# One element cleared by GpSimd between any two gathers of a graph layer

## The chip, the cores and the metric

The kernel runs on one core of a Trainium2 chip. The metric is the device time of one execution in microseconds, as the median of several runs.

## The reference

A graph of 12,500 nodes with 32 features each, and 400,000 edges, sorted by their target `dst`. Two layers, each followed by a layer norm over the 32 features with a residual:

```python
m = relu(x[src] + edge_attr)                         # layer 0: one message per edge
neigh = segment_sum(m, dst)
x = layernorm(x + (1 + eps) * x + neigh)

out_deg, in_deg = clip(count(src), 1), clip(count(dst), 1)   # layer 1
y = x * rsqrt(out_deg)
x = layernorm(x + segment_sum(y[src], dst) * rsqrt(in_deg))
```

## The kernel before

**Layer 0** (`layer_0`) takes the edges in 125 groups of 3200, as 128 partitions by J = 25 edges. Per group the feature rows of the source nodes must come from `x` in HBM. GpSimd fetches them with 25 indirect DMAs (`gathers`, L152): each takes one column of `src_t` (128 row numbers) and fetches 128 rows of 128 bytes into `rows[:, slot, j, :]`. `rows`, `src_t`, `dst_t` and `edge_t` have four slots, so a group uses slot g % 4.

Every engine runs its own program, in steps (`turns`): steps 0 to 3 are written out, then a loop of four steps a turn, then the rest. In step g VectorE and ScalarE work on the gathered rows of group g - 1:

- ScalarE copies the edge features into PSUM (L565), VectorE adds the gathered rows (L412; the first half of the group waits until all 25 gathers of it have landed, `z_rows`), ScalarE applies the relu and splits the sum into bf16 parts with VectorE (L572, L417, L576, L421).
- VectorE makes one-hot matrices from node numbers (`one_hot`, L132): `b_hot` and `key_hot` for the counts that layer 1 needs, `hi_hot` and `lo_hot` for the degree of the sources, `dst_hot` for the targets.
- TensorE multiplies, in this order: 24 products into `built` (L636), each pair of which ScalarE takes away (L587) into `stage` (a part of `big`), 25 for the histogram of sources (L641), and 25 that sum the messages by target into `agg` (L648). The last of these raises `z_agg`.
- SyncE stores `stage` to HBM (`stash`, L514), and every second step loads the indices and edge features of two groups (L489, L491).

GpSimd's own step g waits for the indices of group g, for `z_sum` (the slot of `rows` must have been read), and for `z_agg` to be at least g - 1, which is the end of TensorE's last `agg` product of step g - 1. Then it issues its 25 gathers. So the gathers of group g run beside step g of the other engines, and are used in step g + 1.

**Layer 1** (`layer_1`) has no gather in the usual case: it applies the stored counts with matmuls. GpSimd rests there. `general_sums` is a fall-back for other inputs and is skipped with these.

Of the kernel before, what the change touches and what calls it, by code (L numbers as in the profile page):

```python
# [4 lines left out]
F32, BF16, F16, I32, U32 = mybir.dt.float32, mybir.dt.bfloat16, mybir.dt.float16, mybir.dt.int32, mybir.dt.uint32  # L5
# [4 lines left out]
P = 128  # L10
# [6 lines left out]
def build(nc, x, src, dst, edge, eps, out, table, x1):  # L17
    N, D = x.shape
    E = src.shape[0]
    J = 25  # L20
# [34 lines left out]
    with ExitStack() as ctx:  # L55
        def allocators(stack):
            return (lambda name, shape, dt=F32: stack.enter_context(nc.sbuf_tensor(name, shape, dt)),
                    lambda name: stack.enter_context(nc.psum_tensor(name, [P, 512], F32)))

        sb, pb = allocators(ctx)  # L60

        def sem(name):
            return ctx.enter_context(nc.semaphore(name))
# [36 lines left out]
        s_mark = sem("s_mark")  # L100
# [48 lines left out]
        def gathers(gp, j0, j1, nodes, rows_d, src_d, s):  # L149

            for j in range(j0, j1):
                gp.indirect_dma_start(  # L152
                    rows_d[:, j, :], None, nodes,
                    bass.IndirectOffsetOnAxis(ap=src_d[:, j:j + 1].bitcast(U32), axis=0),
                ).then_inc(s, 16)
# [56 lines left out]
        def layer_0():  # L212
# [5 lines left out]
            def turns(engine, step):  # L218
                for g in range(4):
                    step(g, g, 0)  # L220
                with engine.Fori(0, fours) as i:
                    for slot in range(4):
                        step(i * 4 + (4 + slot), slot, i + 1)
                for g in range(4 + 4 * fours, G + 2):
                    step(g, g % 4, g // 4)

            def builds(g):

                return not isinstance(g, int) or g < G
# [13 lines left out]
            def loaded(engine, s, s_first, slot, use, n):  # L243

                if isinstance(use, int) and use == 1 and slot == 0:
                    engine.wait_ge(s_first, n)
                else:
                    engine.wait_ge(s[slot // 2], use * n)

            with ExitStack() as own:  # L250
                sb, pb = allocators(own)
                src_t = sb("src_t", [P, 4, J], I32)
                dst_t = sb("dst_t", [P, 4, J], I32)
                edge_t = sb("edge_t", [P, 4, J, D])
                rows = sb("rows", [P, 4, J, D])
# [33 lines left out]
                agg_bank = pb("agg")  # L289
                agg, folded = agg_bank[0:R, 0:W], agg_bank[0:DE, W:2 * W]  # L290
                taken = sb("taken", [R, W])
                sum_ps = pb("sum_ps")[:, 0:JA * D].rearrange("p (j d) -> p j d", d=D)
                built = [own.enter_context(nc.psum_tensor(f"built{k}", [P, 2, 512], F32)) for k in range(2)]
                turn = [built[0][:, k, :] for k in range(2)]
# [6 lines left out]
                z_rows = [sem(f"z_rows{k}") for k in range(4)]  # L301
# [81 lines left out]
                with nc.Block() as block:  # L383
# [143 lines left out]
                    @block.gpsimd  # L527
                    def _(gp):

                        for h in range(2):  # L530
                            gp.iota(pick_i[:, h, :], [[1, max(HT)], [0, SPAN]], base=h * HT[0], channel_multiplier=0).then_inc(s_const, 1)

                        def step(g, slot, u):
                            if builds(g):
                                loaded(gp, z_in, z_in0, slot, u + 1, IN)
                                gp.sem_inc(s_mark, 1)
                                if not isinstance(g, int) or g >= 4:

                                    gp.wait_ge(z_sum, g * 2 - 6)
                                    gp.sem_inc(s_mark, 1)  # L540
                                if not isinstance(g, int) or g >= 2:

                                    gp.wait_ge(z_agg, g - 1)
                                    gp.sem_inc(s_mark, 1)
                                gathers(gp, 0, J, x[:, :], rows[:, slot, :, :], src_t[:, slot, :], z_rows[slot])
                        turns(gp, step)

                    @block.scalar
# [677 lines left out]
        with ExitStack() as later:  # L1226
            with nc.psum_tensor("hist", [P, 512], F32) as hist_bank:
                hist = hist_bank[:, 0:C]
                layer_0()
                counts = later.enter_context(nc.sbuf_tensor("counts", [P, 2, HB + 1, C, CS], BF16))  # L1230
                finish_0()
            layer_1()
# [29 lines left out]
```

## Time and profile before

| | |
|---|---|
| median of 3 runs | 6035.83 us (6033.46 to 6036.26) |
| the profiled execution's own time | 6052.44 us |
| its span, from the first to the last instruction | 6050.5 us |
| VectorE, ScalarE, GpSimd busy in the span | 2859.8, 2724.8, 2963.9 us |
| TensorE busy in the span | 3462.7 us |
| share of the span before layer 1's matmuls begin | 4835.94 us of 6050.5 us |

Layer 0 fills about four fifths of the span. There no engine is near full: the time goes in the order in which the engines wait for each other. A row of the profile names the engine, the line of the kernel, the operation with what it writes and reads, how often, the busy time and the time that the engine stood idle before it, with what ended that idle time. "issue" means that nothing that the profile shows held the instruction. PE is TensorE, PEld its weight loads, DVE VectorE, ACT ScalarE, POOL GpSimd, SP SyncE.

### The profile page before, as it was taken

Reading aid. Unit: us, or ns where it says so; the run is one execution under the profiler, and the core shown is the slowest. Engines: PE = TensorE matmul, PEld = TensorE weight load, DVE = VectorE, ACT = ScalarE, POOL = GpSimd, SP = SyncE. Lnnn points to the kernel's source line nnn. Section 1 sums busy time; section 2 is a strip of 40 time slices with the busy share of each in tenths; the row PEclk is TensorE's granted clock in tenths of the full one; section 3 lists DMA queues with packets and bytes.
Section 4 is the critical chain, followed back from the end, with each engine's and each line's share of the span. In section 5 each row is a group of like instructions: output and inputs, shape, how many; then the busy total and the mean of one; then the engine's idle time right before and its main releaser. Section 6 shows DMA issues by size and latency. Waiting matters only on the chain. (4 is left out here: it accounts for less than half of the span.)

```text
span 6050.5 us, 72100 instructions
## 1 busy us (share of the span) xinstructions
PE 3462.7 (57%) x24270; PEld 1940.1 (32%) x24270; DVE 2859.8 (47%) x4229; ACT 2724.8 (45%) x2908; POOL 2963.9 (49%) x3134
## 2 busy tenths in 40 slices
PE   3444444444444444444444444444444499999998
PEld 1111111111111111111111111111111288888887
DVE  5444444444444444444444444444444544444444
ACT  3444444444444444444444444444444355555553
POOL 5666666666666666666666666666666300000000
PEclk7555555555555555555555555555555599999998
DMA  3232333333323333333232333333333389999996
GB/s 106 85 104 100 100 102 102 102 102 102 102 99 105 101 102 101 101 102 103 98 105 100 101 102 102 102 102 102 102 102 112 126 287 325 323 326 324 326 326 223
DMA packets 272749, 867.67 MB, mean 143 GB/s; under 512 B 93830, under 2 KB 143830, under 8 KB 256214
## 3 DMA queue, kind: packets, MB, share of 16 engines
q1 hardware_dynamic: 172718, 815.90, 36.3%
q0 software_dynamic: 100000, 51.40, 5.8%
q8 instruction: 16, 0.26, 0.0%
q14 instruction: 15, 0.11, 0.0%
HBM read 486.74 MB, written 380.33 MB: 143 GB/s over the span
## 5 line engine op out<-in xcount | busy, mean ns | idle before, releaser
L152 POOL DMA_INDIRECT rows<-in_x,src_t x3125 | 2962.2, 948 | 1806.7 <-issue 914.1
L587 ACT ACTIVATE big<-built 128x980 bf16<-128x980 f32 x1500 | 1790.6, 1230 | 2445.6 <-PE built L636 2298.7
L636 PE MATMUL built<-key_hot,b_hot 100*128 100x490 bf16 x3000 | 1475.6, 603 | 603.1 <-ACT big L587 308.2
L648 PE MATMUL agg<-dst_hot,msg 128*97 128x128 bf16 x3125 | 510.2, 289 | 1842.4 <-issue 1841.1
L412 DVE TENSOR_TENSOR sum_ps<-sum_ps,rows 128x416 f32<-128x416 f32 x250 | 144.2, 577 | 1999.4 <-DMA rows<-in_x,src_t 1994.1
L648 PEld LDWEIGHTS agg<-dst_hot,msg 128*97 128x97 bf16 x3125 | 379.7, 181 | 1955.8 <-issue 1953.6
L828 PE MATMUL applied<-counts,x_parts 128*96 128x160 bf16 x12250 | 916.8, 233 | 1.4 <-ACT counts L786 1.4
L828 PEld LDWEIGHTS applied<-counts,x_parts 128*96 128x96 bf16 x12250 | 880.8, 123 | 65.0 <-ACT counts L786 2.3
L132 DVE TENSOR_TENSOR key_hot<-iota_ps,hk_g 100x3920 bf16<-100x3920 f16 x375 | 820.8, 2189 | 0.0
L636 PEld LDWEIGHTS built<-key_hot,b_hot 100*128 100x128 bf16 x3000 | 232.8, 116 | 1699.3 <-issue 896.8
L786 ACT ACTIVATE counts<-built 128x980 bf16<-128x980 f32 x500 | 598.5, 1238 | 391.8 <-PE built L814 391.6
L417 DVE SCALAR_TENSOR_TENSOR sum_ps<-sum_ps,msg 128x416 f32<-128x416 f32 x250 | 144.2, 577 | 378.4 <-ACT msg L572 378.4
L132 DVE TENSOR_TENSOR b_hot<-iota_ps,hk_g 100x1024 bf16<-100x1024 f16 x375 | 257.9, 688 | 99.6 <-issue 76.1
L814 PE MATMUL built<-big,hi_hot 100*128 100x490 bf16 x1000 | 272.9, 374 | 32.7 <-DVE big L132 26.4
L641 PEld LDWEIGHTS hist<-lo_hot,hi_hot 128*128 128x128 bf16 x3125 | 268.5, 144 | 67.8 <-issue 64.0
L641 PE MATMUL hist<-lo_hot,hi_hot 128*128 128x98 bf16 x3125 | 275.8, 281 | 3.4 <-DVE lo_hot L132 3.4
L132 DVE TENSOR_TENSOR big<-iota_ps,hk_g 100x3920 bf16<-100x3920 f16 x125 | 273.6, 2189 | 0.0
L132 DVE TENSOR_TENSOR dst_hot<-iota_ps,rel 128x3200 bf16<-128x3200 f16 x125 | 226.7, 1814 | 0.1
L132 DVE TENSOR_TENSOR hi_hot<-iota_ps,s_hi 128x3200 bf16<-128x3200 f16 x125 | 226.7, 1814 | 0.0
L752 DVE CAST slots<-small 80x64 bf16<-80x64 f32 x125 | 27.6, 220 | 369.0 <-PE small L839 369.0
L132 DVE TENSOR_TENSOR lo_hot<-iota_ps,s_lo 128x2450 bf16<-128x2450 f16 x125 | 178.0, 1424 | 0.0
L572 ACT ACTIVATE msg<-sum_ps 128x416 bf16<-128x416 f32 x250 | 124.9, 500 | 93.7 <-DVE sum_ps L412 74.8
(130 smaller groups left out, 1543.4 us busy)
## 6 DMA issues: line engine op xcount, KB each, us to landing
stash<-big SPq DMA_DIRECT2D x125, 2940.0 KB
counts<-stash SPq DMA_DIRECT2D x250, 1470.0 KB, 8.7
rows<-in_x,src_t POOLq DMA_INDIRECT x3125
edge_t<-in_edge_attr SPq DMA_DIRECT2D x61, 800.0 KB
big<-in_dst SPq DMA_DIRECT2D x1, 1562.5 KB
big<-in_src SPq DMA_DIRECT2D x1, 1562.5 KB
src_t<-in_src SPq DMA_DIRECT2D x61, 24.8 KB
dst_t<-in_dst SPq DMA_DIRECT2D x61, 24.8 KB
```

The lines of the kernel that those rows point to most:

```text
L132: return ve.tensor_tensor(out.rearrange("p n (w t) -> p n w t", t=2), row[0:p, 0:w].rearrange("p (w t) -> p w t", t=2).unsqueeze(1).to_bro ...
L152: gp.indirect_dma_start(rows_d[:, j, :], None, nodes, bass.IndirectOffsetOnAxis(ap=src_d[:, j:j + 1].bitcast(U32), axis=0),).then_inc(s, 16)
L412: ve.tensor_tensor(half(h), half(h), rows[:, prev, j0:j1, :], ALU.add).then_inc(z_sum, 1)
L417: ve.scalar_tensor_tensor(half(h), half(h), 0.0, part(0, h), ALU.max, ALU.subtract).then_inc(z_left, 1)
L572: sc.activation(part(0, h), half(h), ACT.Relu).then_inc(z_part0, 1)
L587: sc.activation(stage[:, slot % 2, q, :, d0:d0 + 2 * SPAN].rearrange("p c (b d) -> p b c d", b=2), built[n % 2][:, :, 0:KEYS].rearrange("p ...
L636: last = te.matmul(built[n % 2][:, b, 0:KEYS], b_hot[:, r, t, :], key_hot[:, r, t, :], start=True, stop=True)
L641: last = te.matmul(hist[:, :], hi_hot[:, j, :], lo_hot[:, j, :], start=False, stop=False)
L648: last = te.matmul(agg, msg[:, j, 0:R], dst_hot[:, j, :], start=(j == 0), stop=(j == J - 1))
L786: sc.activation(counts[:, slot, HB, :, d0:d0 + 2 * SPAN].rearrange("p c (b d) -> p b c d", b=2), built[n % 2][:, :, 0:KEYS].rearrange("p b ...
L814: last = te.matmul(built[n % 2][:, b, 0:KEYS], hi_hot[:, slot, t, :], key_hot[:, slot, t, :], start=True, stop=True)
L828: last = te.matmul(applied[slot].rearrange("m (q d) -> m q d", d=CS), x_parts[:, c, :], counts[:, other, :, c, :], start=(c == 0), stop=(c ...
```

## The change

Layer 0's step on GpSimd issues its 25 gathers one by one, and after each a `memset` of one bf16 element in each of the 128 partitions of a new buffer `rest`, at column j. Each `memset` raises a new semaphore `z_rest`. Before its gathers, a group from the second on waits until all `memset`s of the groups before it are done. What is gathered, and when a group may begin, is otherwise as before.

```diff
@@ layer_0, buffers
                 taken = sb("taken", [R, W])
+                rest = sb("rest", [P, J], BF16)
+                z_rest = sem("z_rest")
@@ layer_0, GpSimd's step
                                     gp.wait_ge(z_agg, g - 1)
                                     gp.sem_inc(s_mark, 1)
-                                gathers(gp, 0, J, x[:, :], rows[:, slot, :, :], src_t[:, slot, :], z_rows[slot])
+                                if not isinstance(g, int) or g >= 1:
+
+                                    gp.wait_ge(z_rest, g * J)
+                                    gp.sem_inc(s_mark, 1)
+                                for j in range(J):
+
+                                    gathers(gp, j, j + 1, x[:, :], rows[:, slot, :, :], src_t[:, slot, :], z_rows[slot])
+                                    gp.memset(rest[:, j:j + 1], 0.0).then_inc(z_rest, 1)
```

## Rows read from the trace of the kernel before

**Rows 1.** The page: busy us of each engine, share of the span, instructions.
```profile
PE 3462.7 (57%) x24270; PEld 1940.1 (32%) x24270; DVE 2859.8 (47%) x4229; ACT 2724.8 (45%) x2908; POOL 2963.9 (49%) x3134
```

**Rows 2.** The waits, whole span: engine, line, waited for: us in total, times, longest.
```profile
DVE sum_ps L412 <- DMA rows<-in_x,src_t: 1994.1, 123, 18.4
PE agg L648 <- issue: 1841.1, 1041, 3.2
POOL rows L152 <- PE agg L648: 887.8, 123, 44.8
```

**Rows 3.** Groups of instructions on POOL from 164 to 4744 us.
```profile
L152 POOL DMA_INDIRECT rows<-in_x,src_t x3026 | 2858.8, 945 | 1727.9 <-issue 884.9 <-PE agg L648 843.1
```

**Rows 4.** Timeline of POOL: start us, us, instruction, idle before and releaser.
```profile
126.24 0.95 POOL L152 DMA_INDIRECT rows<-in_x,src_t  x1 [44.76 <-PE agg L648]
...
2019.67 0.94 POOL L152 DMA_INDIRECT rows<-in_x,src_t  x1 [6.68 <-PE agg L648]
2020.92 0.95 POOL L152 DMA_INDIRECT rows<-in_x,src_t  x1 [0.30 <-issue]
...
2049.66 0.95 POOL L152 DMA_INDIRECT rows<-in_x,src_t  x1 [0.30 <-issue]
2057.68 0.94 POOL L152 DMA_INDIRECT rows<-in_x,src_t  x1 [7.07 <-PE agg L648]
...
4742.97 0.94 POOL L152 DMA_INDIRECT rows<-in_x,src_t  x1 [6.41 <-PE agg L648]
```

**Rows 5.** Timeline of PE, the end of one step.
```profile
2035.60 2.25 PE L641 MATMUL hist<-lo_hot,hi_hot 128*128 128x98 bf16 x25
2037.65 0.84 PE L648 MATMUL agg<-dst_hot,msg 128*97 128x128 bf16 x6
2039.83 0.27 PE L648 MATMUL agg<-dst_hot,msg 128*97 128x128 bf16 x1 [1.34 <-issue]
...
2053.33 0.27 PE L648 MATMUL agg<-dst_hot,msg 128*97 128x128 bf16 x1 [1.83 <-issue]
2055.43 1.44 PE L648 MATMUL agg<-dst_hot,msg 128*97 128x128 bf16 x12 [1.83 <-issue]
```

**Rows 6.** Timeline of PE, the first such products, and some of the preparation.
```profile
77.00 1.07 PE L367 MATMUL built<-ident,big 125*100 125x125 f32 x4 [2.46 <-issue]
...
123.31 2.12 PE L648 MATMUL agg<-dst_hot,msg 128*97 128x128 bf16 x25
```

**Rows 7.** Timeline of DVE about the same step.
```profile
2036.11 0.55 DVE L421 TENSOR_TENSOR msg<-sum_ps,msg 128x384 bf16<-128x384 f32 x1
2053.55 0.60 DVE L412 TENSOR_TENSOR sum_ps<-sum_ps,rows 128x416 f32<-128x416 f32 x1 [16.89 <-DMA rows<-in_x,src_t]
```

**Rows 8.** Stretches: us, busy by engine, granted clock, DMA share, GB/s.
```profile
2044.00:2048.00 4.00, 0.53 (x2) 0.32 (x2) 0.00 (x0) 0.00 (x0) 3.08 (x4) 0.50 0.93 382
2084.00:2088.00 4.00, 0.27 (x1) 0.32 (x2) 0.00 (x0) 0.00 (x0) 3.09 (x4) 0.50 0.10 16
4820.00:6050.00 1230.00, 1177.70 (x14598) 1033.01 (x14598) 593.32 (x1281) 656.32 (x636) 0.00 (x0) 0.97 0.86 304
```

**Rows 9.** DMA queues from 400 to 4600 us: packets, MB, share.
```profile
q0 software_dynamic: 88736, 45.61, 7.3%
q14 instruction: 1, 0.01, 0.0%
```

**Rows 10.** Timeline of POOL before the first gather.
```profile
0.31 0.12 POOL L1246 MEMSET const-bfloat16-1.0<- 128x1 bf16 x1
0.34 0.12 POOL L1246 MEMSET const-uint8-127<- 128x1 uint8 x1
0.85 0.23 POOL L172 IOTA x_parts<- 128x128 int32 x1 [0.40 <-PEq L169]
1.05 0.12 POOL L173 IOTA col_i<- 128x1 int32 x1
```

**Rows 11.** Timeline of all engines in the preparation, beside early gathers.
```profile
44.03 3.49 DVE L334 TENSOR_TENSOR big<-big,c_first 125x3200 f32<-125x3200 int32 x1
44.60 4.78 POOL L152 DMA_INDIRECT rows<-in_x,src_t  x1 [0.30 <-issue]
```

**Rows 12.** Groups on DVE from 164 to 4744 us, the copies.
```profile
L391 DVE COPY hk_g<-hk_all 100x96 f16 x116 | 24.4, 210 | 3.7
```

## The prediction

> **What bounds the kernel now.** I read the page's busy times first. No engine is busy for more than 57% of the span [rows 1], so it is an order of waits that sets the time, and the waits say which. VectorE stands idle for 1994.1 us until the gathered rows are there, in 123 pieces; GpSimd, which gathers them, stands idle for 887.8 us until TensorE's last `agg` product, in 123 pieces too; and TensorE has 1841.1 us of idle time ahead of its `agg` products that nothing in the profile explains [rows 2]. These three make a ring. The timelines show one turn of it. Gathers start 1.25 us apart (2019.67, 2020.92: 0.95 of work, 0.30 of pause) and 25 of them take from 2019.67 to 2050.61, 30.94 us. GpSimd then rests 7.07 us until 2057.68 [rows 4]. In the meantime TensorE does its histogram at full pace (25 products in 2.25 us), then six `agg` products, and then goes over to one product in about 2.1 us, from 2039.83 to 2053.33 (seven of them); at 2055.43 the last twelve come in 1.44 us, to 2056.87 [rows 5]. GpSimd goes on 0.81 us later.
>
> A turn is thus 30.94 us of gathers, 4.82 us until TensorE runs free again, 1.44 us of products, 0.81 us of hand-over: 38.01 us, which is 2057.68 - 2019.67. Over the layer the first gathers of a group stand at 126.24 us (group 2) and 4742.97 us (group 124) [rows 4], 122 turns of 37.84 us on average; 30.93 of that is gathering, for GpSimd's wait is 843.1 us in 122 turns, 6.91 us each [rows 3].
>
> What slows the `agg` products is the open point. With no gather running, the same 25 products took 2.12 us at 123.31 us [rows 6]. Slow stretches are equally slow with the DMA engines at 0.93 and at 0.10 of their time, and in layer 1, without a gather, TensorE stays busy (1177.70 of 1230 us) with the DMA engines at 0.86 [rows 8]. So DMA load does not do it; GpSimd's gathering goes with it, in the preparation too (2.46 us ahead of four transposes while early gathers run [rows 6]). The granted clock is 0.50 of full speed (1.2 GHz) in both slow stretches [rows 8], but a half clock doesn't make gaps of two microseconds.
>
> A rule bears on this. The Trainium skill, Runtime: NRT & Kernel Launch, section "Instruction fetch mechanics", says that an engine's instructions are fetched by DMA in 16 KiB blocks, and that a taken branch whose target is not at hand waits for one. By it the slow products would be waiting for blocks, GpSimd's pace would have no part in it, and the time would go by the full chain alone. The trace disagrees: from 400 to 4600 us one instruction packet was moved [rows 9]. I give it no part in the sum.
>
> **The change, part by part.**
>
> *3125 memsets.* Each stands between two gathers in GpSimd's own order, and no other engine waits for it. Its cost on the path is what it adds to the 1.25 us from gather to gather; call it d. The trace has no memset behind a gather. Below: four memsets at the program's start lie 0.03 us apart (0.31, 0.34), each 0.12 us long [rows 10], and if the memset ran wholly inside the 0.30 us pause that stands before each gather [rows 4], d would be 0. It can hardly be under that, since the number of gathers and the 0.95 us of each stay. Above: the memset in full and a second pause, 0.12 + 0.30 = 0.42 us. I take 0.12 us, the memset's own row [rows 10] set end to end with the gather: a one-element iota after another instruction also shows 0.12 and no pause (1.05 [rows 10]). A group's gathers then take 25 x 0.12 = 3.0 us more, 33.9 us.
>
> *What happens with these 3.0 us.* I read the release of TensorE as tied to the end of gathering: in the turn above it comes 4.82 us after the last gather and 1.88 us after VectorE starts again at 2053.55 [rows 5, 7], and VectorE itself waits for the last gather to land. If this tie holds, the turn is the gathers plus the same 7.07 us, and all of the 3.0 us shows: 122 x 3.0 = 366 us. Group 124 is the last; its rows come 3.0 us later, and VectorE waits for them: 3 us. Groups 0 and 1 are gathered ahead of the ring, while VectorE still prepares, and GpSimd then waits 44.76 us [rows 4]; their 6 us are hidden by that.
>
> *The new wait on `z_rest`.* The last memset of a group is over about 7 us before the next group begins (the wait for `agg` covers it). Behind the wait only the gathers are queued. If the cover went, it would cost one memset, 0.12 us a group, 15 us. I take 0, with the semaphore increment beside it.
>
> *VectorE and the memset.* When VectorE worked on large buffers in the preparation, one gather took 4.78 us instead of 0.95, beside an instruction of 3.49 us [rows 11]; in the loop the mean is 945 ns [rows 3], so its VectorE work doesn't hold gathers up. The Trainium skill, SBUF — State Buffer, section "Who interferes with whom", says that copies in a two-port mode and GpSimd take a shared port in turn, whole instructions at a time. By it a memset that meets the copy of `hk_g` (210 ns [rows 12]) would wait for its end, at most once a group: 122 x 0.21 = 26 us on top. No row of the loop shows a gather so held.
>
> *Sum.* 366 + 3 = 369 us. Against the profiled execution's 6052.44 us that is 6421 us. That execution is 16.6 us above the median of the runs, so I put the median at 6405 us.
>
> **Rivals.**
>
> *The rest frees TensorE (faster).* The place is the slow stretch of the `agg` products. Suppose that gathers at 1.25 us overload something by a little: it would fill up for some time, slow TensorE, and need a while to drain after the last gather. For it: the six or seven fast products ahead of the slow ones, and the 4.82 us of drain after 30.94 us of gathers [rows 4, 5], which would be an excess of 15%, so that a pace slower by 0.19 us a gather would do away with it, and one slower by 0.12 us might put off its start past the last product, which needs only two more microseconds. Then `agg` is over long before the gathers, GpSimd is bound by itself, and the turn is 25 x (1.25 + 0.12) + 0.2 = 34.4 us: (37.84 - 34.4) x 122 = 420 us less, 5616 us. The point from which it decides: the slow stretch must be gone, and d below 6.6 / 25 = 0.26 us; beyond that the gathers alone take longer than the turn of now. Against it: TensorE stays slow for 4.8 us after GpSimd has stopped altogether [rows 4, 5], so that a pause of a tenth of a microsecond should free nothing. 0.29.
>
> *Only half shows.* The ring goes over two groups: from a step's first addition (2053.55 [rows 7]) to its `agg` end is some 42 us, and the gathers and the hand-over stand for the rest of two turns. If TensorE's release hangs on that chain rather than on the gathers' end, two turns grow by 3.0 us: 183 us more, 6219 us. Against it speaks the sudden release at 2055.43, for which I see nothing but the end of the gathers. 0.13.
>
> *A second pause.* The memset brings a pause of its own, d = 0.42: 10.5 us a group, 123 x 10.5 = 1292 us, 7328 us. Or d lies between, at 0.3: 6958 us. A slow dispatch would work like it: in the slow stretch TensorE's instructions come in steps of about 0.7 us (weight load and product, 2.1 us a pair at most [rows 5]), and were GpSimd's two instructions held to such a step, a pair would take 1.4 us, d = 0.15, close to what I took. 0.12.
>
> *Nothing on the path.* The memset lies in the 0.30 us pause: 6036 us. It would need d under 0.004 us to be within the bound below. 0.07.
>
> **How the numbers follow.** The forecast has 0.39. With its own spread of d (0.05 to 0.2 us: 154 to 615 us more) it reaches from 6190 to 6650 us. The case of a freed TensorE ends at 5616 us, or 5590 with a d of nearly 0.1; I take it in. Above, d = 0.28 gives 6897 us; beyond lies under a tenth. Range 5590 to 6900 us. What a measurement of this kernel can tell from no change is 0.2%, 12 us. Faster by more: 0.29. Within: 0.07. Slower by more: 0.39 + 0.13 + 0.12, 0.64.
>
> **What would show it.** In the timeline of GpSimd the distance from gather to gather: 1.37 us by the forecast, 1.25 if nothing shows, 1.67 with a second pause. GpSimd's wait for `agg` a group: still 6.9 us by the forecast, 5.4 if half shows, 0 if TensorE is freed. In TensorE's timeline the single `agg` products 2.1 us apart: one or two more of them by the forecast, and fewer in the burst at the end; all 25 in one row of some 2 us if it is freed. The distance of that burst from the last gather: 4.8 us if the tie holds. VectorE's wait for rows a group: 16 us now, 19 by the forecast. I am wrong if the distance from gather to gather grows and the wait for `agg` goes down by more than it grows.

## The result

The changed kernel takes 6076.46 us (median of 3 runs, 6076.15 to 6076.52) against 6035.83 us: 40.6 us more, ratio 1.0068 with a 95% interval of 1.0048 to 1.0088. The direction is the one forecast, the size is a ninth of it (369 us).

The page of the changed kernel, busy us of each engine and the costliest groups on GpSimd (in the groups: busy us, mean ns | idle before):

```profile
PE 3449.3 (57%) x24270; PEld 1937.3 (32%) x24270; DVE 2866.8 (47%) x4229; ACT 2723.6 (45%) x2908; POOL 3321.5 (55%) x6259
...
L152 POOL DMA_INDIRECT rows<-in_x,src_t x3125 | 2957.5, 946 | 1458.9 <-PE agg L657 826.4
...
L554 POOL MEMSET rest<- 128x1 bf16 x3125 | 374.9, 120 | 14.1 <-issue 12.8
```

The 3125 memsets are there, 120 ns each as taken, and GpSimd is 358 us busier [rows 1]. But the idle time ahead of the gathers fell by about as much (1458.9 us, 1806.7 before on the page's row for L152): the memsets lie in it. The timeline shows how:

```profile
1994.42 0.95 POOL L152 DMA_INDIRECT rows<-in_x,src_t  x1 [0.19 <-issue]
1995.37 0.12 POOL L554 MEMSET rest<- 128x1 bf16 x1
1995.67 0.94 POOL L152 DMA_INDIRECT rows<-in_x,src_t  x1 [0.19 <-issue]
```

From gather to gather it is 1.25 us, as before [rows 4]: the 0.12 us of memset came out of the 0.30 us pause. So the cost that I put on the path isn't there, and something else takes the 40 us. Two places stand out. One gather in some groups is late, always near the end of a group, and the profile shows no wait that held it:

```profile
1983.63 0.94 POOL L152 DMA_INDIRECT rows<-in_x,src_t  x1 [0.19 <-issue]
1984.56 0.13 POOL L554 MEMSET rest<- 128x1 bf16 x1
1986.00 0.94 POOL L152 DMA_INDIRECT rows<-in_x,src_t  x1 [1.32 <-issue]
1986.95 0.12 POOL L554 MEMSET rest<- 128x1 bf16 x1
1993.17 0.94 POOL L152 DMA_INDIRECT rows<-in_x,src_t  x1 [6.11 <-PE agg L657]
```

That was so for the last gather in 56 groups (1.21 us of idle time ahead of it on average, 0.19 otherwise) and for the one before it in 12, and in no group before the change. The other place is the preparation: TensorE's transposes and ScalarE's copies, which hand over to each other while the first 50 gathers run, got slower (2.46 us ahead of four transposes in [rows 6]). TensorE after the change:

```profile
77.71 1.07 PE L369 MATMUL built<-ident,big 125*100 125x125 f32 x4 [4.60 <-issue]
84.02 1.07 PE L369 MATMUL built<-ident,big 125*100 125x125 f32 x4 [5.24 <-ACT hk_all L561]
```

The ring then begins at 129.97 us, 3.7 us later than in [rows 4]. A turn is 38.006 us on average (122 turns), 0.164 more than 37.842, 20 us in all; gathers take 31.44 us of it (30.93 before), GpSimd's rest 6.56 (6.91). These two profiled executions differ by 24.1 us only (6076.52 against 6052.44); the one of before was 16.6 us above its median.

One memset was itself held up, in the preparation and not in the ring. It took 1.78 us, and ended with an instruction of VectorE (49.24 + 1.83 is 51.07 us):

```profile
49.24 1.83 DVE L338 TENSOR_SCALAR x_parts<-x_parts 125x3200 f32<-125x3200 f32 x1
49.32 1.78 POOL L554 MEMSET rest<- 128x1 bf16 x1
49.63 2.25 POOL L152 DMA_INDIRECT rows<-in_x,src_t  x1
```

The next gather starts at 49.63 us all the same (49.69 before the change), so nothing was lost by it on GpSimd. In the ring no memset took more than 0.17 us.

TensorE's slow stretch is still there, as in [rows 5]:

```profile
2011.01 0.84 PE L657 MATMUL agg<-dst_hot,msg 128*97 128x128 bf16 x6
2012.31 0.26 PE L657 MATMUL agg<-dst_hot,msg 128*97 128x128 bf16 x1 [0.46 <-issue]
2015.14 0.22 PE L657 MATMUL agg<-dst_hot,msg 128*97 128x128 bf16 x1 [2.57 <-issue]
...
2028.48 1.50 PE L657 MATMUL agg<-dst_hot,msg 128*97 128x128 bf16 x12 [0.46 <-issue]
```

### The profile page after: what moved, and what is told of

It reads as the page before. It is cut to its first block and busy times, and to the rows that moved or that the text cites. A ratio compares the mean times of both kernels' runs of the same rounds, so it can differ in the third digit from the quotient of the medians.

```text
span 6074.5 us, 75465 instructions
## 1 busy us (share of the span) xinstructions
PE 3449.3 (57%) x24270; PEld 1937.3 (32%) x24270; DVE 2866.8 (47%) x4229; ACT 2723.6 (45%) x2908; POOL 3321.5 (55%) x6259
## 5 line engine op out<-in xcount | busy, mean ns | idle before, releaser
L152 POOL DMA_INDIRECT rows<-in_x,src_t x3125 | 2957.5, 946 | 1458.9 <-PE agg L657 826.4
L554 POOL MEMSET rest<- 128x1 bf16 x3125 | 374.9, 120 | 14.1 <-issue 12.8
```

Source lines behind the costliest of these rows:

```text
L152: gp.indirect_dma_start(rows_d[:, j, :], None, nodes, bass.IndirectOffsetOnAxis(ap=src_d[:, j:j + 1].bitcast(U32), axis=0),).then_inc(s, 16)
L554: gp.memset(rest[:, j:j + 1], 0.0).then_inc(z_rest, 1)
```

## The experiments

The theory formed from this (A): while GpSimd gathers, every engine's instructions arrive slowly, after some that it had in hand, and each further instruction that GpSimd takes makes it worse for all. The rival (B): the memset's work costs. Each of the five sets of runs below was made on one chip, with the kernel before beside it, and the chips turned out to differ: the kernel before took 5976, 6011 and 5976 us on three of them and 5228 and 5237 us on two. I call these chips of the first and of the second kind; the executions above show the first.

### First chip: what costs, work or count

e1_again is the change itself. The others replace the memset line behind each gather:

```diff
 e2_count_only
-    gp.memset(rest[:, j:j + 1], 0.0).then_inc(z_rest, 1)
+    gp.sem_inc(z_rest, 1)
 e3_two_memsets (waits for 2 * J a group)
+    gp.memset(rest[:, 2 * j:2 * j + 1], 0.0).then_inc(z_rest, 1)
+    gp.memset(rest[:, 2 * j + 1:2 * j + 2], 0.0).then_inc(z_rest, 1)
 e4_long_memset (from group 2 on; 188 elements of x_parts, idle then)
+    gp.memset(x_parts_flat[:, j * 188:(j + 1) * 188], 0.0).then_inc(z_rest, 1)
```

> The changed kernel itself, again, beside the kernel before on one chip. The two profiled executions differ by 24 us (20 in the ring of layer 0, 3.7 ahead of the first ring turn), the medians by 40.6 us. If the profiles tell the whole effect, the medians here differ by 20 to 30 us; if the unprofiled runs have a second cost, by 35 to 45 us.

> Instead of each memset GpSimd's queue holds a plain semaphore increment: as many instructions more (25 a group), but no work for the engine. Theory A, instruction count: what costs is that GpSimd takes more instructions while gathers run, and all engines get theirs slowly then; so this costs about what the change costs (15 to 45 us), the preparation's transposes stretch as in the changed kernel (first ring turn at about 130 us, not 126), and the last gather of every second group comes over 1 us late. Theory B, the memset's own work: the time is that of before, within 12 us, and the first ring turn at 126 us.

> Two memsets of one element behind each gather, 50 a group. If the pause of 0.30 us ahead of a gather swallows whatever fits in it, the distance from gather to gather stays 1.25 us (0.94 + 0.12 + 0.12 + what is left). If 0.19 us ahead of a gather is a fixed pause, it goes to 1.37 us and the turn grows by up to 3 us, 370 us in all. Theory A (count) adds: more late gathers, from earlier in the group, and the first ring turn later than 130 us; at least twice the change's 24 to 40 us.

> The same number of instructions as the change, but from the third group on each memset clears 188 bf16 elements of each partition (an idle buffer), by the iota rows some 0.3 us instead of 0.12. If memset and pause overlap, the distance from gather to gather is 1.25 to 1.3 us and the time that of the change; if the 0.19 us ahead of a gather is fixed, the distance is about 1.43 us and the gathers of a group take 4.5 us more: by the tie that I predicted (release of TensorE 4.8 us after the last gather) 4.5 x 122 = 550 us more than the change; if a slower pace frees TensorE, the turn is 36 us and the time about 250 us less than before.

| kernel | us | ratio (95%) | turn | gathers | rest |
|---|---|---|---|---|---|
| before | 5975.9 | | | | |
| e1_again | 6011.3 | 1.0060 (1.0047 to 1.0074) | 37.48 | 31.26 | 6.22 |
| e2_count_only | 6017.2 | 1.0069 (1.0056 to 1.0083) | 37.57 | 30.94 | 6.63 |
| e3_two_memsets | 5916.1 | 0.9902 (0.9887 to 0.9917) | 36.67 | 33.39 | 3.28 |
| e4_long_memset | 5866.8 | 0.9818 (0.9805 to 0.9832) | 36.28 | 34.25 | 2.04 |

Turn, gathers and rest are means over 122 turns of the timeline of GpSimd, from the first gather of group 2 to that of group 124. The kernel before was not traced on this chip; h1_before, traced on another chip with the same 5976 us, has 37.22, 30.90 and 6.32 us.

The change costs 35.4 us here, at the lower edge of the 35 to 45 expected if the two profiles above hid part of it. e2 bears on work against count: semaphore increments, with no work for the engine, cost at least as much as the memsets (41.3 us), so the memset's work is not needed for a cost of this size. That it is the same cost isn't shown: with increments the rest grows (6.63 us) and the gathers don't (30.94), with memsets the gathers grow (31.26), by the late ones. For the preparation it says the opposite of what A expected: with increments the ring began at 126.47 us, as before, with memsets at 129.67 us. And no late gathers appeared in e2.

In e3 both memsets fit in the pause, 0.03 us apart, and the distance stays 1.25 us, as the first of its expectations had it:

```profile
2004.57 0.12 POOL L555 MEMSET rest<- 128x1 bf16 x1
2004.84 0.94 POOL L152 DMA_INDIRECT rows<-in_x,src_t  x1 [0.16 <-issue]
2005.79 0.12 POOL L554 MEMSET rest<- 128x1 bf16 x1
2005.81 0.12 POOL L555 MEMSET rest<- 128x1 bf16 x1
2006.09 0.94 POOL L152 DMA_INDIRECT rows<-in_x,src_t  x1 [0.16 <-issue]
```

But GpSimd's own instructions now come late from the 15th to 17th gather of a group on, the gathers take 33.4 us, and yet the turn is shorter and the time 59.8 us less, where theory A had at least twice the change's cost on top. e4 shows the same without that detour. Its memset is longer than the pause can hold, the distance is 1.39 us (0.95 + 0.27 + 0.17), and the turns alternate between 35.3 and 37.3 us. In one of the two TensorE has nearly all its products at once:

```profile
2067.95 1.52 PE L658 MATMUL agg<-dst_hot,msg 128*97 128x128 bf16 x21
2069.82 0.22 PE L658 MATMUL agg<-dst_hot,msg 128*97 128x128 bf16 x1 [0.35 <-issue]
2070.53 0.33 PE L658 MATMUL agg<-dst_hot,msg 128*97 128x128 bf16 x3 [0.49 <-issue]
```

So a slower pace of the gathers does free TensorE in part, as my rival had it; the memset of the change is only too short to slow them. The turn is the 36 us that e4's last expectation named; the gain is 109 us and not 250.

### Second chip: another machine

```diff
 f2_memsets_behind
+    gathers(gp, 0, J, ...)
+    for j in range(J):
+        gp.memset(rest[:, j:j + 1], 0.0).then_inc(z_rest, 1)
 f3_count_twice
+    gp.sem_inc(z_rest, 1)      # two such lines behind each gather
+    gp.sem_inc(z_rest, 1)
 f4_pause_mid_group (long from group 2 on)
+    gathers(gp, 0, 12, ...)
+    gp.memset(x_parts_flat[:, 0:3700], 0.0).then_inc(z_rest, 1)
+    gathers(gp, 12, J, ...)
```

> The kernel before itself, for a trace on the same chip as the three that follow. Chips differ by about 1% with the same kernel, so the turn of layer 0's ring, 37.84 us in the first trace, may be 37.2 to 37.9 us here; the pattern (30.9 us of gathers, 25 of them 1.25 us apart, then some 6.5 us of rest) stays.

> The 25 memsets of a group all behind its last gather, none between gathers. Theory A (the number of instructions that GpSimd takes counts): some 30 to 40 us more than before, as with memsets between or with semaphore increments. Rival (what counts is something between gathers): the time of before within 12 us, since the 25 memsets (3 us at 0.12) fit in GpSimd's rest of 6.5 us.

> Two semaphore increments behind each gather, 50 a group, no memset. With one, the time went up by 41 us, 0.33 us a turn. Theory A: with two it goes up by about twice as much, 70 to 100 us, and the rest before each group grows. Rival: the distance between gathers is what counts and stays at 1.25 us, so no more than the 41 us of one.

> No memset behind each gather, but one long one (3700 bf16 elements of each partition, 0.81 ns an element by the 188-element memset: 3.1 us) after the 12th gather of each group from the third on: a rest in the middle instead of small ones. Theory C (TensorE's instructions come slowly while gathers run at 1.25 us, and a rest of any kind lets it catch up): TensorE reaches its agg products about 18 us after the group's first gather with more in hand, the slow stretch shortens by several products, the turn is 34.5 to 37 us and the time 100 to 350 us less than before. Rival (the release hangs on the end of the gathers): the turn grows by the whole pause, 3 us, 370 us more.

| kernel | us | ratio (95%) | turn | gathers | rest |
|---|---|---|---|---|---|
| f1_before | 5228.3 (5227.7 beside) | 1.0001 (0.9991 to 1.0011) | 31.22 | 30.91 | 0.31 |
| f2_memsets_behind | 5410.1 | 1.0350 (1.0336 to 1.0365) | 32.73 | 30.91 | 1.82 |
| f3_count_twice | 5227.3 | 1.0000 (0.9991 to 1.0009) | 31.22 | 30.91 | 0.31 |
| f4_pause_mid_group | 5604.7 | 1.0722 (1.0708 to 1.0737) | 34.29 | 33.99 | 0.31 |

These expectations were made for a chip of the first kind, and here theory A fails in f2 and f3. The rivals of f3 (no more than 41 us) and f4 (3 us a turn, 370 us more) have the right figures, but for another reason. The kernel before has no slow stretch here although the gathers run beside it, and GpSimd alone is the bound, with gathers back to back. TensorE in f1_before:

```profile
2034.46 2.25 PE L641 MATMUL hist<-lo_hot,hi_hot 128*128 128x98 bf16 x25
2036.51 2.41 PE L648 MATMUL agg<-dst_hot,msg 128*97 128x128 bf16 x25
```

50 increments a group cost nothing. Real time on GpSimd costs: the long memset takes 3.20 us and lengthens the turn by 3.07, the 25 in a row take 0.80 us and lengthen it by 1.51, since the next gather then waits for VectorE (1.45 us in f2's timeline).

### Third chip, of the first kind: how much the count costs

> The changed kernel, on another chip. Two kinds of chip have shown up: on two of them the turn of the ring is 37.5 to 38 us and TensorE's agg products come 2.1 us apart beside gathers, on a third the same kernel before has a turn of 31.22 us, 25 gathers back to back, and all 25 agg products in 2.6 us. On a chip of the first kind: 30 to 45 us more than before. On one of the second kind, where two semaphore increments a gather cost nothing: a distance of 1.25 us between gathers as before, so within 12 us of before if the memset hides in the pause.

> Two semaphore increments behind each gather. On a chip of the second kind they cost nothing (5227.3 against 5227.7 us). On one of the first kind, theory A (the number of instructions that GpSimd takes while gathers run is paid by TensorE's pace): twice the 41 us of one increment, 70 to 100 us. Rival: no more than the 41 us.

> One memset of 3700 elements after the 12th gather of a group. On a chip of the second kind it costs its whole 3.07 us a turn, 375 us. On one of the first kind, theory C (any rest lets TensorE's instructions catch up): 50 to 350 us less than before. Rival (the release hangs on the end of the gathers): 3 us a turn, 370 us more.

> The indirect gathers are left out: SyncE loads 3200 rows of x in order with one DMA a group instead, with GpSimd's waits (so the result is another one; TensorE, VectorE and ScalarE do the same work). If gathering is what slows TensorE's instructions on a chip of the first kind, its 25 agg products take 2 to 3 us here on any chip, and the turn is what the other engines need, 24 to 30 us. Rival (something else of that chip slows them, whatever GpSimd does): single agg products 2 us apart remain.

The first three are the change, f3's and f4's kernels. g4 takes the gathers away, so its result is another one; SyncE loads as many rows in order instead, and VectorE waits for that load:

```diff
 g4_no_gathers, SyncE (the gathers on GpSimd left out)
+    sp.wait_ge(z_sum, g * 2 - 6); sp.wait_ge(z_agg, g - 1)
+    sp.dma_start(rows[:, slot, ...], x[0:GE, :]...).then_inc(z_rows[slot], 16)
```

| kernel | us | ratio (95%) | turn | gathers | rest |
|---|---|---|---|---|---|
| before | 6011.0 | | | | |
| g1_change | 6056.6 | 1.0076 (1.0063 to 1.0089) | 37.82 | 31.31 | 6.51 |
| g2_count_twice | 6095.2 | 1.0141 (1.0126 to 1.0155) | 38.18 | 31.06 | 7.12 |
| g3_pause_mid_group | 6002.9 | 0.9988 (0.9977 to 0.9999) | 37.55 | 33.98 | 3.57 |
| g4_no_gathers | 3904.5 | 0.6495 (0.6486 to 0.6505) | | | |

Two increments a gather cost 84 us where one cost 41 on the first chip. The cost goes with the count, though by how much isn't exact: one increment was not measured on this chip, where the change too costs more (45.5 us against 35.4). TensorE has fewer products before the slow ones begin, four or five instead of six or seven with the change on the same chip, and more left for the burst (14 instead of 12):

```profile
2054.59 0.63 PE L658 MATMUL agg<-dst_hot,msg 128*97 128x128 bf16 x4
2057.16 0.27 PE L658 MATMUL agg<-dst_hot,msg 128*97 128x128 bf16 x1 [1.94 <-issue]
...
2072.56 1.72 PE L658 MATMUL agg<-dst_hot,msg 128*97 128x128 bf16 x14 [0.44 <-issue]
```

Late gathers, which e2 did not have, show in 8 groups here, with no memset at all.

The long pause in the middle left the time nearly where it was (8 us less; its 12 runs lie between 5988 and 6020 us, those of the change within 3 us of each other). That is neither theory's figure, and the means in the table hide what happened: in 61 of the 122 turns g3 needs 34.3 us, in the other 61 it needs 40.8 on average, and the two kinds nearly always alternate. In the short ones TensorE has all its products at once, and GpSimd alone is the bound; in the long ones it is as slow as ever:

```profile
2009.78 3.20 POOL L552 MEMSET x_parts<- 128x3700 bf16 x1
2023.82 0.63 PE L656 MATMUL agg<-dst_hot,msg 128*97 128x128 bf16 x4
2026.72 0.22 PE L656 MATMUL agg<-dst_hot,msg 128*97 128x128 bf16 x1 [2.27 <-issue]
...
2050.69 3.19 POOL L552 MEMSET x_parts<- 128x3700 bf16 x1
2053.91 2.47 PE L656 MATMUL agg<-dst_hot,msg 128*97 128x128 bf16 x25
```

The products come at once where they begin as the pause ends (2053.88 us), and slowly where they begin 10.8 us after its end (2012.98). So a pause does let TensorE catch up, as theory C had it, when it lies just ahead of the products; that the next turn loses it again is why C's 50 us didn't come. The rival, by which every turn grows with the gathers, is refuted.

Without gathers, on this same chip, the slow stretch is gone:

```profile
2010.39 2.25 PE L649 MATMUL hist<-lo_hot,hi_hot 128*128 128x98 bf16 x25
2012.44 2.50 PE L656 MATMUL agg<-dst_hot,msg 128*97 128x128 bf16 x25
2024.68 0.64 PE L629 MATMUL agg<-taken,fold_r 97*33 97x128 f32 x2
```

Turns are 20.5 us apart (2010.39, 2030.88), less than expected. So it is the gathering that slows TensorE's instructions, on this chip and, as the traces look alike, on chips of this kind.

### Fourth chip, of the first kind: where the instructions stand

```diff
 h3_ring_only (its wait counts from group 2)
+    if not isinstance(g, int) or g >= 2:
+        gp.memset(rest[:, j:j + 1], 0.0).then_inc(z_rest, 1)
 h4_no_wait_for_agg (kernel before)
-    gp.wait_ge(z_agg, g - 1)
-    gp.sem_inc(s_mark, 1)
```

> The kernel before, for a trace on the same chip. First kind of chip: turn 37.2 to 37.9 us, slow agg products. Second kind: 31.22 us.

> The 25 memsets behind the last gather of the group. They come when the gathers are over, so on a chip of the first kind they are short of the slow stretch: if only instructions taken between gathers cost, the time is that of before within 12 us; if their number counts wherever they stand, 30 to 45 us more. On the second kind 182 us more, as measured (1.5 us a turn, nothing to hide behind).

> The memsets only from the third group on; groups 0 and 1 are gathered as before. On a chip of the first kind the first turn of the ring begins where it does before (126 us instead of 130 or 131), and the total is 3 to 5 us below that of the changed kernel: 0.5 to 0.7% over before. If the preparation were not where those 3 to 5 us are, the ring would begin as late as in the changed kernel. On the second kind no difference, within 12 us.

> GpSimd does not wait for agg: gathers run ahead until their slot of rows is free, which the wait for z_sum still guards. On a chip of the second kind 31.2 us a turn as before. On the first kind, theory A: gathers need 31 us of a turn at all events and TensorE's instructions catch up only when they pause, so the turn does not come down to 31 us; it stays at 36 us or more, and the time within 4% of before, or above. Rival: the wait itself makes the turn long, and without it GpSimd alone sets it, 31.2 us, 750 us less.

| kernel | us | ratio (95%) | turn | gathers | rest |
|---|---|---|---|---|---|
| h1_before | 5976.8 (5976.4 beside) | 1.0000 (0.9990 to 1.0010) | 37.22 | 30.90 | 6.32 |
| h2_memsets_behind | 5995.1 | 1.0031 (1.0019 to 1.0044) | 37.34 | 30.90 | 6.44 |
| h3_ring_only | 6008.0 | 1.0053 (1.0039 to 1.0067) | 37.49 | 31.22 | 6.27 |
| h4_no_wait_for_agg | 6861.6 | 1.1482 (1.1464 to 1.1499) | 44.49 | 30.90 | 13.59 |

h3 against h1 is the change's ring by itself: 0.27 us a turn, 33 us in 122 turns, against 31.6 us between the medians. All of it lies in the gathers (31.22 us against 30.90), by late ones in 47 groups. Its ring begins at 126.32 us, so the 3 to 5 us of the preparation are the memsets of groups 0 and 1.

Behind the gathers the memsets cost 18.7 us, between the two expectations, and 0.12 us a turn of it lies in the ring (14 us), 3 us in the preparation (the ring begins at 129.32 us). What is of most use is how they run, GpSimd in h2:

```profile
2026.85 0.63 POOL L553 MEMSET rest<- 128x1 bf16 x19
2028.28 0.10 POOL L553 MEMSET rest<- 128x1 bf16 x1 [0.80 <-issue]
2028.98 0.10 POOL L553 MEMSET rest<- 128x1 bf16 x1 [0.60 <-issue]
2030.38 0.10 POOL L553 MEMSET rest<- 128x1 bf16 x1 [1.30 <-issue]
```

19 of them in 0.63 us, and then one every 0.70 or 1.40 us: after 25 gathers and 19 memsets, 44 instructions, GpSimd falls into the same steps as TensorE in [rows 5]. In the changed kernel it is the 47th or 49th gather or memset of a group that comes late, in e3 mostly the 45th to 49th. This looks like one and the same thing on both engines: a number of instructions in hand, then one in 0.7 us or a multiple. It is not shown to be. Semaphore increments would have to count less than memsets, for e2 has 50 gathers and increments a group and none late, and g2 has 75 with a late one in few groups.

h4 shows what the wait for `agg` is good for. Without it most of the slow stretch lies in the products into `built`, where gathers now run beside them: TensorE's idle time there that nothing explains is 2238.8 us, 307.7 in h1. A step of TensorE's, and GpSimd's wait for indices, in which TensorE catches up:

```profile
2018.80 1.00 PE L632 MATMUL built<-key_hot,b_hot 100*128 100x490 bf16 x2 [3.96 <-ACT big L583]
2030.70 1.00 PE L632 MATMUL built<-key_hot,b_hot 100*128 100x490 bf16 x2 [10.90 <-issue]
2036.24 1.00 PE L632 MATMUL built<-key_hot,b_hot 100*128 100x490 bf16 x2 [4.54 <-ACT big L583]
2037.03 2.25 PE L637 MATMUL hist<-lo_hot,hi_hot 128*128 128x98 bf16 x25
```

```profile
2057.49 0.94 POOL L152 DMA_INDIRECT rows<-in_x,src_t  x1 [27.09 <-DMA dst_t<-in_dst]
```

It is 14.8% slower. By this reading the rest of 6 to 7 us a turn is not lost time on such a chip; it is when the engines' instructions catch up.

### Fifth chip, of the second kind: slower pace on purpose

```diff
 i1_every_second (both from group 2 on)
+    if j % 2 == 1:
+        gp.memset(x_parts_flat[:, j * 376:(j + 1) * 376], 0.0).then_inc(z_rest, 1)
 i2_long_120
+    gp.memset(x_parts_flat[:, j * 120:(j + 1) * 120], 0.0).then_inc(z_rest, 1)
```

> A memset of 376 bf16 elements (0.42 us) after every second gather, from the third group on. The gathers of a group take about 34 us, as with 188 elements behind each, with half as many instructions more. Theory C with theory A (mean pace frees TensorE, count of instructions loads it): at least as good as that kernel, 1.8 to 3% less than before on a chip of the first kind. Rival (each gather needs its own pause): less gained, under 1%. On a chip of the second kind the gathers alone set the turn: 2.9 us a turn, 350 us more, 6 to 7%.

> A memset of 120 bf16 elements (about 0.22 us) behind each gather: the distance is about 1.33 us, as with two small memsets (1.0% less than before), but with half their instructions. Theory A and C: better than those, 1.2 to 2% less, and worse than or equal to 188 elements (1.8%). Rival (only the pace counts): 1.0% as with two small ones. On a chip of the second kind 2 us a turn, 4 to 5% more.

i1 took 5669.4 us against 5236.5, ratio 1.0826 (1.0811 to 1.0841), turn 34.81 us; i2 took 5558.8 us, 1.0616 (1.0601 to 1.0630), turn 33.93. With no slow stretch to cure, the pause is all cost, more than I expected by 1 to 2%: i2's gathers take 32.90 us and its rest 1.02 instead of 0.31, and i1 has 3.6 us more of gathers where I had 2.9. i2's distance is 1.33 us (0.95 + 0.22 + 0.16). i1's 3.6 us are 12 memsets of 0.43 us less 0.13 us each, as the long memset cost 0.13 us less than it took. What they would do on the first kind stays open, and so does the best spacing. No version tried beats the kernel before on both kinds: e4 gains 1.8% on the first, and kernels that pace the gathers like it lose 6 to 8% on the second.

## Why the prediction was wrong, step by step

- **What bounds the kernel:** the ring of three was read rightly for the first kind of chip, gathers, slow `agg`, hand-over. That gathering slows TensorE was argued from rows and is now shown on one chip (g4: 25 products in 2.50 us without gathers on a chip that has the slow stretch with them). On the second kind the ring doesn't exist.
- **"I take 0.12 us, the memset's own row set end to end with the gather":** this is the step that failed. The memset's 0.12 us stands in the 0.30 us pause, d is 0 within 0.01 us (1.25 us between gathers). The lower bound of the range of d was the truth; I had the nearest row for the memset's length and none for where it lies. The pause gives room for about 0.13 us, an estimate from these rows: 0.12 us leaves 0.19 of it and the distance as it was, 0.22 and 0.27 us leave 0.16 to 0.17 and make the distance 1.33 and 1.39 us, and 3.20 us lengthen the turn by 3.07.
- **"If this tie holds, the turn is the gathers plus the same 7.07 us":** it doesn't. In the changed kernel the gathers take 0.51 us more a turn and the turn 0.16. In e4, with a d of 0.14 us, the gathers take 3.35 us more than in h1 and the rest falls by 4.3, which is what the prediction named as its sign of being wrong. Had d been 0.12 us, the 366 us would still have been wrong: e4 gains 109 us. What the release of TensorE hangs on instead isn't shown in full; a pause just ahead of its products does it (g3).
- **The missing term:** 25 more instructions a group. I priced GpSimd's instructions by their time only. By h3 they cost 0.27 us a turn, 33 us, and 3 to 5 us in the preparation, where I had put 0 ("their 6 us are hidden by that"). Sum 36 to 38 us, against 35.4, 40.6 and 45.5 us measured in three comparisons. e2 and g2 show that 25 and 50 instructions without work cost 41 and 84 us, so count alone can make a cost of this size; that the memsets' cost, which lies in late gathers, is the same one is argued. It is 0.01 us for each instruction, which no row for a memset could have told.
- **The wait on `z_rest`:** 0, as put, as far as the timeline shows: GpSimd's first gather of a group follows TensorE's `agg`.
- **VectorE and the memset:** the 26 us that the prediction set beside its sum did not come. In the ring of the changed kernel one memset ran beside a copy of `hk_g` and none took more than 0.17 us, for the copies come before a group's gathers. A memset was held for 1.78 us once, in the preparation, beside a `tensor_scalar` of VectorE.
- **The rivals:** "nothing on the path" (0.07) had the mechanism right and missed the count. "The rest frees TensorE" (0.29) describes a real effect that this memset is too short for. It showed at 1.35 us between gathers in the mean (e3, 1.0%) and at 1.39 us (e4, 1.8%); between 1.27 us, the changed kernel's mean, and 1.35 nothing was tried on such a chip. The gain is not the 7% that I worked out, because half the turns still take 37.3 us and the others 35.3, not 34.4. Its lower end was also added up wrongly: by its own sum a d of 0.1 us gives about 5560 us, not 5590. "Only half shows" and "a second pause" did not happen.

Not settled: why the preparation suffers from memsets (129.67 to 131.32 us) and hardly from increments (126.47, 127.08), why late gathers are many with memsets (45 to 56 groups) and none or few with increments, why the long and short turns of g3 and e4 alternate, what the two kinds of chip differ in, and what it is in a gather that holds back the others' instructions. The changed kernel itself did not run on a chip of the second kind; there the distance of 1.25 us and the free increments of f3 speak for no difference, which is argued only.

## What to carry to other kernels

Before pricing a small instruction between two long ones on a queue, look for the pause that already stands ahead of the long one: what fits in it is free, and only what goes beyond it counts. Where a row says "issue" for microseconds on one engine, count the instructions that all engines take in that stretch, not only their time, since an instruction without work can cost as much as one with. Look at turns one by one before trusting their mean: g3's 37.55 us is half 34.3 and half 40.8. And measure the kernel before on the same chip: here the choice of chip moved it by 13%, twenty times the effect, and turned a gain of 1.8% into a loss of 6 to 8% for the same idea.

## What the runs showed of the hardware

- One program without any change runs at 5228 to 5237 us on two chips, at 5976 to 6011 us on three, and at 6036 us in the first comparison. Nearly all of the difference is in the stretch with indirect gathers (turn 31.22 against 37.2 to 37.8 us), and with none of them the one chip so tried gives 3904.5 us.
- On the slower ones, instructions beside gathers come in steps of 0.70 us, seen on TensorE and on GpSimd itself, which in h2 runs some 44 gathers and memsets of a group at the usual pace first. The Trainium skill, Runtime: NRT & Kernel Launch, "Instruction fetch mechanics", says that a taken branch can make an engine wait for the fetch of a 16 KiB block; the single instruction packet in the loop [rows 9] and the single steps don't look like it.
- A memset of one element takes 0.12 us on GpSimd, but the next may begin 0.03 us later; 188 and 120 bf16 elements of each partition take 0.27 and 0.22 us.
- A memset of one element on GpSimd beside a `tensor_scalar` of VectorE on 3200 f32 elements of each partition took 1.78 us instead of 0.12 and ended with it.
